# First stage of a two-layer kernel with its tiles started three ahead, small-tile mixing and logits, and GpSimd's bias after both sums of the tile before

## The reference

```
att   = softmax(mlp(cond))                 # 32 x 8, a small net on 128 values per batch
agg_w = sum_k att[b,k] * weight[k]         # a 64 x 64 mixing matrix for each batch
y     = agg_w @ x[b] + (att @ bias_k)      # mixes the 64 rows of a batch
g     = softmax(y @ gate_w.T)              # 8 routing weights for each row
u     = y * (g @ in_channel_scale)
x1    = x + u @ sign(weight).T * (g @ out_channel_scale) + bias
```

## Time and profile before

| | us |
|---|---|
| median of 3 runs | 580.35 (579.39 to 580.51) |
| the profiled execution | 579.01 |
| its span | 576.9 |

### The profile page before, as it was taken

The page is one execution under the profiler, slowest core; times in us unless marked ns, Lnnn a source line. Parts: engine busy times, 40 slices in busy tenths (PEclk is TensorE's granted clock), DMA queues, the critical chain, the costliest instruction groups (busy, mean ns, idle before and its releaser), DMA issues.

```text
span 576.9 us, 12309 instructions
## 1 busy us (share of the span) xinstructions
PE 562.8 (98%) x4917; PEld 491.0 (85%) x4917; DVE 253.1 (44%) x478; ACT 119.2 (21%) x271; POOL 148.3 (26%) x79
## 2 busy tenths in 40 slices
PE   4899999999999999999999999999999999999997
PEld 3778888888888889889889889899898898898896
DVE  4486567766676467242233222422422422323231
ACT  4723324323333233011010111111110110111100
POOL 0245555456453648011011011010110110110100
PEclk9999999999999999999999999999999999999999
DMA  8805333253333595223123043032131240330100
GB/s 333 324 36 164 111 119 118 86 178 92 112 118 111 158 192 151 78 39 110 45 77 113 32 83 105 9 114 82 32 114 52 61 114 36 77 111 9 68 36 36
DMA packets 36178, 58.22 MB, mean 101 GB/s; under 512 B 4096, under 2 KB 24384, under 8 KB 36160
## 3 DMA queue, kind: packets, MB, share of 16 engines
q1 hardware_dynamic: 36016, 57.70, 32.6%
q10 hardware_dynamic: 144, 0.26, 0.1%
HBM read 41.15 MB, written 16.79 MB: 100 GB/s over the span
## 4 chain that ended last, share of the span: by engine, by line
PE 93%; DVE 1%; ACT 0%; issue 0%
PE bank L503 50%; PE bank L430 20%; PE bank L482 8%; PE bank L383 4%; PE bank L392 4%; PE bank L538 4%; PE bank L406 1%; PE bank L398 0%; PE bank L531 0%; PE bank L412 0%; DVE weighted L738 0%; DVE agg L743 0%; DVE work L767 0%; DVE work L897 0%; ACT routing L617 0%; ACT gate L612 0%
## 5 line engine op out<-in xcount | busy, mean ns | idle before, releaser
L503 PE MATMUL bank<-early,parts 128*128 128x320 f32 (+1 forms) x1152 | 206.6, 337 | 0.0
L503 PEld LDWEIGHTS bank<-early,parts 128*128 128x128 f32 x1152 | 184.7, 188 | 16.6
L430 PE MATMUL bank<-late,parts 128*128 128x512 f32 x512 | 133.2, 407 | 1.8 <-ACT parts L628 1.5
L430 PEld LDWEIGHTS bank<-late,parts 128*128 128x128 f32 x512 | 92.6, 191 | 21.8 <-ACT parts L628 1.9
L954 POOL TENSOR_TENSOR work<-work,bias_bc 128x1024 f32<-128x1024 f32 x16 | 39.0, 2440 | 278.1 <-DMA work<-x_scratch 278.1
L503 PE MATMUL bank<-late,parts 128*128 128x512 f32 x384 | 94.3, 394 | 0.0
L503 PEld LDWEIGHTS bank<-late,parts 128*128 128x128 f32 x384 | 70.9, 188 | 16.1
L628 ACT ACTIVATE parts<-work 128x512 fp32r<-128x512 f32 x64 | 39.8, 632 | 102.3 <-DVE work L847 65.1
L922 POOL TENSOR_TENSOR work<-work 128x512 f32<-128x512 f32 x32 | 41.3, 1290 | 51.4 <-DVE work L803 51.4
L795 DVE TENSOR_TENSOR parts<-work,parts 128x512 fp32r<-128x512 f32 x64 | 46.6, 750 | 12.2 <-ACT parts L628 10.6
L914 POOL TENSOR_TENSOR work<-xs,bias_bc 128x1024 f32<-128x1024 f32 x16 | 38.8, 2428 | 47.4 <-ACT late L605 24.3
(11 more groups left out here) (89 smaller groups left out, 351.3 us busy)
## 6 DMA issues: line engine op xcount, KB each, us to landing
xs<-in_x SPq DMA_DIRECT2D x16, 512.0 KB, 3.8
x_scratch<-work SPq DMA_DIRECT2D x16, 512.0 KB, 3.0
raw<-x_scratch SPq DMA_DIRECT2D x128, 64.0 KB, 3.2
work<-x_scratch SPq DMA_DIRECT2D x16, 512.0 KB, 3.6
out_tokens<-work SPq DMA_DIRECT2D x15, 512.0 KB, 2.7
stage<-in_wearly SPq DMA_DIRECT2D x8, 576.0 KB, 3.8
row_bc<-token_rows_scratch SPq DMA_DIRECT2D x30, 64.0 KB, 3.6
work<-in_wsign SPq DMA_DIRECT2D x3, 512.0 KB, 10.9
```

The lines of the kernel that those rows point to most:

```text
L430: last = mm(bank[4 + h][:, :], parts[:, p, a, c, :], signs[:, c, h * HALF:(h + 1) * HALF], start=(k % 16 == 0), stop=(k % 16 == 15))
L503: return mm(dst, parts[:, p, a, c, :], w(b, c), start=(k == 0), stop=(close and k == 23))
```

## The change

- **Depth.** PE's period of tile t now does, in one block before step 18 (BLOCK_AT): logits of t+2, y of t+3, scales of t+1. The turn stands before step 7, the sum of the logits of t+2 before step 26. `y_t` has two buffers of its own. The first period is written out; DVE's and ACT's lists follow the new order, with mix_kernels four tiles ahead.
- **Small-tile mixing.** `agg` is 128 x 64: each batch's matrix on its 64 rows. product_y makes 32 matmuls of 64x64 with 64 columns (block c, batch b, column half g) in place of 8 of 128x128. Bank b now holds batch b, so the bias is added batch by batch. mix_kernels has one reduce.
- **Logits.** The gate, padded to 32 columns, is stationary; 128 columns of y_t move. Blocks c and c+4 go to the column tile c % 4, so bank 2 has four partial sums; ACT copies them (`logits_t`) and one matmul with the selection matrix C_SEL adds and turns them (`sum_logits`).
- **x again.** resid is loaded with x from DRAM (`load_again`) after x1 of two tiles before has been stored; add_bias0 works in place, and on POOL it stands after make_x1 of the tile before, both halves. make_x1 goes half by half.
- **Start.** The constants come in three transfers, one on ACT's queue; sign chunks, scales and x of tile 1 come in another order; SP's transfers around the first stage's end are put in another order (weight pieces, raw loads of the convolution, x1 of the last tiles).

The diff, cut to its core (of most parts only the new and the kept lines; what they replace stands in the functions above):

```diff
+TURN_AT, BLOCK_AT, SUM_AT, CONV0_AT = 7, 18, 26, 8
+SIGNS_FIRST = 4
...
+        agg = sb("agg", [P, 2, S])
...
+            load_consts(0, C_W0, C_W1)
             sp.dma_start(rws[:, :], rows).then_inc(rows_loaded, 16)
+            load_consts(2, C_GATE, C_END)
             load_x(0, 0)
+            for c in range(3):
+                load_sign(c)
             sp.dma_start(bias_bc[:, 0:HALF], scales).then_inc(scales_loaded, 16)
+            load_sign(3)
             load_x(0, 1)
+            for c in range(4, L8):
+                load_sign(c)
+            sp.wait_ge(tok_rows_ready, 2)
+            sp.dma_start(rows_dram.rearrange("a b s -> b a s"), tok_rows[:, :, :]).then_inc(rows_stored, 16)
+            def load_next(i, p, biased):
+                sp.wait_ge(y_biased, biased)
+                load_x(i, p)
+                load_row(aggb_row, i, p, aggb_loaded)
+            def load_again(i, p):
+                sp.dma_start(resid[:, p, :], tile_rows(x, 2 * i + p)).then_inc(x_again_loaded[p], 16)
+            sp.wait_ge(rows_stored, 16)
+            load_next(1, 0, 2)
+            for p in range(2):
+                sp.wait_ge(signs_ready, 7 + p)
+                load_again(0, p)
             sp.wait_ge(scale_ready, 1)
             sp.dma_start(bias_bc[:, :], bias0.broadcast_to([P, H])).then_inc(bias0_loaded, 16)
+            load_next(1, 1, 4)
...
+            def replace_x1(i, p):
+                store_x1(i, p)
+                sp.wait_ge(x1_stored[p], 16 * (i + 1))
+                load_again(i + 1, p)
+            def next_chunk(i):
                 sp.wait_ge(stage_hi[0], i + 1)
                 sp.wait_ge(stage_lo[0], i + 1)
                 load_stage(0, wearly[:, bass.ds(i + 1, 1), :].rearrange("p a n -> p (a n)"), NW)
+            with sp.Fori(0, PAIRS - 3) as i:
+                load_next(i + 2, 1, 4 * i + 8)
+                replace_x1(i, 0)
+                next_chunk(i)
+                load_next(i + 3, 0, 4 * i + 10)
+                replace_x1(i, 1)
+            late_i, last = PAIRS - 3, PAIRS - 1
+            load_next(last, 1, 4 * late_i + 8)
+            replace_x1(late_i, 0)
+            next_chunk(late_i)
+            replace_x1(late_i, 1)
...
+            replace_x1(last - 1, 0)
+            next_chunk(last - 1)
...
+            replace_x1(last - 1, 1)
             sp.wait_ge(xb_ready, 2 * TILES)
             sp.dma_start(bias_bc[:, :], bias1.broadcast_to([P, H])).then_inc(bias1_loaded, 16)
+            store_x1(last, 0)
+            store_x1(last, 1)
...
+            def inputs_of_y(i, p):
+                pe.wait_ge(x_loaded[p], 16 * (i + 1))
+                pe.wait_ge(agg_ready, 2 * i + p + 1)
             def product_y(i, p):
                 for c in range(L8):
+                    for b in range(2):
+                        for g in range(2):
+                            at = c * P + g * S
+                            rows = slice(b * S, (b + 1) * S)
+                            made = mm(bank[b][g * S:(g + 1) * S, c * S:(c + 1) * S], xs[rows, p, at:at + S],
+                                      agg[rows, p, :], start=True, stop=True)
+                        if c == L8 - 1:
+                            made.then_inc(y_done, 1)
+            def product_logits(i, p, first_tile=False):
+                pe.wait_ge(y_biased, 4 * i + 2 * p + 2)
+                if not first_tile:
+                    pe.wait_ge(gate_exp, 2 * i + p)
+                for c in range(L8):
+                    at = slice(EP * (c % 4), EP * (c % 4) + EP)
+                    made = mm(bank[2][at, 0:P], cst[:, C_GATE + c * EP:C_GATE + (c + 1) * EP], y_t[:, p, c, :],
+                              start=(c < 4), stop=(c >= 4))
+                made.then_inc(logits_made, 1)
+            def sum_logits(i, p, first_tile=False):
+                pe.wait_ge(logits_copied, 2 * i + p + 1)
+                if not first_tile:
+                    pe.wait_ge(u_ready, 4 * i + 2 * p - 1)
+                mm(bank[2][:, 0:E], logits_t[:, :], cst[:, C_SEL:C_SEL + E], start=True, stop=True).then_inc(logits_done, 1)
...
+            def period0(i, p, one, two=None, three=None):
                 for k in range(32):
                     if k == TURN_AT:
+                        turn_routing(*one)
+                    if k == BLOCK_AT:
+                        if three:
+                            inputs_of_y(*three)
+                        if two:
+                            product_logits(*two)
+                        if three:
+                            product_y(*three)
+                        product_scales(*one, copied=2 if two else 1)
+                    if k == SUM_AT and two:
+                        sum_logits(*two)
+                    ffn0_step(i, p, k)
+            for k in range(32):
+                if k == 6:
+                    pe.wait_ge(u_ready, 1)
+                    product_logits(0, 1)
+                if k == 10:
+                    inputs_of_y(1, 0)
+                    sum_logits(0, 1)
+                    product_y(1, 0)
+                if k == 16:
+                    turn_routing(0, 1)
+                if k == 22:
+                    inputs_of_y(1, 1)
+                    product_logits(1, 0)
+                    product_y(1, 1)
+                    product_scales(0, 1, copied=2)
+                if k == 28:
+                    sum_logits(1, 0)
+                ffn0_step(0, 0, k, True)
+            period0(0, 1, (1, 0), (1, 1), (2, 0))
+            with pe.Fori(1, PAIRS - 2) as i:
+                period0(i, 0, (i, 1), (i + 1, 0), (i + 1, 1))
+                period0(i, 1, (i + 1, 0), (i + 1, 1), (i + 2, 0))
             last_i = PAIRS - 1
+            period0(last_i - 1, 0, (last_i - 1, 1), (last_i, 0), (last_i, 1))
+            period0(last_i - 1, 1, (last_i, 0), (last_i, 1))
+            period0(last_i, 0, (last_i, 1))
...
+            def period0(i, p, one, two=None, chunk=None):
+                if one:
+                    round_routing(*one)
+                copy_out_scale(i, p, 1)
+                if chunk is not None:
+                    round_stage(0, NW, (chunk + 1) * 16, early[:, 0, bass.ds(chunk, 1), :].rearrange("p a n -> p (a n)"))
+                if two:
+                    copy_logits(*two)
+                if one:
+                    round_u(*one)
+                if two:
+                    gate_exps(*two)
+                    spread_routing(*two)
+                if one:
+                    copy_out_scale(*one, 0)
+            period0(0, 1, (1, 0), (1, 1), 0)
...
+                v.tensor_reduce(agg[:, p, :], weighted[:, :, :], AX.X, ALU.add).then_inc(agg_ready, 1)
...
+            add_mix_bias(0, 0, True)
+            dve.wait_ge(scale_hi, 1)
+            v.scalar_tensor_tensor(scale_w[:, :], bias_bc[:, 0:HALF], cst[:, C_SLO:C_SLO + 1], scale_w[:, :].bitcast(F32),
+                                   ALU.mult, ALU.add).then_inc(scale_ready, 1)
+            mix_kernels(0, 1)
+            route_max(0, 0)
+            route_sum(0, 0)
             split_routing(0, 0)
             scale_in(0, 0)
+            rest_of_u(0, 0, 0)
+            add_mix_bias(0, 1, True)
+            rest_of_u(0, 0, 1)
+            mix_kernels(1, 0)
+            route_max(0, 1)
+            route_sum(0, 1)
+            mix_kernels(1, 1)
+            add_mix_bias(1, 0)
+            split_routing(0, 1)
+            scale_out(0, 0, 0)
+            scale_in(0, 1)
+            rest_of_u(0, 1, 0)
+            route_max(1, 0)
+            rest_of_u(0, 1, 1)
+            route_sum(1, 0)
+            add_mix_bias(1, 1)
+            mix_kernels(2, 0)
+            def period0(i, p, before, one, two=None, three=None, four=None):
+                scale_out(*before, 1)
+                split_routing(*one)
+                if four:
+                    mix_kernels(*four)
+                scale_out(i, p, 0)
+                scale_in(*one)
+                rest_of_u(*one, 0)
+                if two:
+                    route_max(*two)
+                rest_of_u(*one, 1)
+                if two:
+                    route_sum(*two)
+                if three:
+                    add_mix_bias(*three)
+            period0(0, 1, (0, 0), (1, 0), (1, 1), (2, 0), (2, 1))
...
-            def add_bias0(i, p, first_tiles=False):
-                pool.wait_ge(x_loaded[p], 16 * (i + 1))
-                if not first_tiles:
-                    pool.wait_ge(x1_stored[p], 16 * i)
-                g.tensor_tensor(resid[:, p, :], xs[:, p, :], bias_bc[:, :], ALU.add).then_inc(xb_ready, 2)
-            def make_x1(i, p):
+            def add_bias0(i, p):
+                pool.wait_ge(x_again_loaded[p], 16 * (i + 1))
+                g.tensor_tensor(resid[:, p, :], resid[:, p, :], bias_bc[:, :], ALU.add).then_inc(xb_ready, 2)
...
+            def period0(before, now, chunk=None):
+                make_x1(*before, 1)
+                add_bias0(*now)
+                if chunk is not None:
```

(36 more changed lines are left out.)

293 lines of the change are left out of this document (112 added, 181 removed).

## The result

The changed kernel takes 559.3 us (median of 4 runs, 558.18 to 560.6) against 579.87 (4 runs): ratio 0.9667, 95% interval 0.9639 to 0.9694. Run again later on another chip beside the experiments it gave 0.9650 (0.9622 to 0.9678). I had predicted 556 and a range of 546 to 570. The profiled execution is 558.58, its span 556.5; before, 579.01 and 576.9: 20.4 less, where 24.2 were predicted.

What follows compares the result with a forecast made beforehand. PE, busy 98% of the span, bounds the kernel. First stage 52 + 11 x 10.04 + 8.9 + 8.05 + 10.2 + 2.0 = 191.6 us against 215.77, 24.2 less: 556 us, range 546 to 570.

Steps and rivals of the forecast that it cites:

- The block: PE's first-stage period with small-tile y and logits, sum, scales and gaps: 10.04 us against 11.84, 1.80 less; bounds 9.5 and 11.2.
- Why y is 1.0: Mixing product on PE: 16 instructions per quarter x (53 streaming + 9 leftover ns) = 1.0 us; bounds 0.85 and 1.42.
- Changes of shape: PE gaps between tile shapes: full to logits 0.30 us, logits to y 0.15, y to scales 0.12; bounds 0 and 0.3 each.
- The first feed-forward step: Start of the first stage: first feed-forward step at 26.7 us, against 26.31 before.
- Periods 0 and 1: First two tile periods: 13.6 and 11.3 us, together to 51.6, taken as 52; bounds 49 and 56.
- the wait of 1.2 for DVE: Period 0: PE waits 1.2 us for DVE's bias of tile 1 and mix of tile 2, on top of 12.35 of work.
- The steady tiles: Tiles 2 to 12 of the first stage: 11 periods of 10.04 us.
- Tile 13: First-stage tile without a y: 8.9 us.
- Tiles 14 and 15: Last first-stage tiles: 8.05 us for 14, which has no logits, and 10.2 for PE's 32 steps and convolution in 15.
- The end: Second stage waits 2.0 us (bounds 0 and 4): x comes late behind 16 raw loads, then bias and last chunk on POOL.
- That the others keep up: DVE's 7.4 us fits in 10.04; ACT slack 0.85 in chunk tiles, POOL at most 7.6 in a row, SP slack 2.6.
- slack 3.9: POOL's bias behind the predecessor's second sum: ACT's copy of the next out-scale to T+10.1, wanted by DVE at T+14.0; hidden.

Runs made afterwards that it cites:

- the other order: Changed kernel with the 32 small matmuls of y reordered, all 16 of one batch, then all of the other: ratio 0.9836 against the kernel before.
- the scales moved apart: Changed kernel with the scales at step 20, two feed-forward steps behind the block: 559.73 us, ratio 0.9679, against 557.95 of the change beside it.
- the move of x: Changed kernel with x1 of tile 13 stored and x of tile 15 loaded after the first eight raw loads, not all sixteen: 555.78 us, ratio 0.9596.
- the copy first: Changed kernel with ACT copying the logits before it rounds the weight chunk, in tiles that carry one: 563.45 us, ratio 0.9717.
- the bias first: Changed kernel with GpSimd's bias of a tile before the second sum of the tile before, not after both: 571.74 us, ratio 0.9862.

## Why the prediction was right, step by step

- *The block.* y 1.09 with its way to the scales (1.0 + 0.12 predicted), logits with the gap behind them 0.58 (0.46 + 0.15), gap ahead 0.32 (0.30), scales 0.59, sum 0.33 (0.24). Period 10.13 against 10.04, where the sum was mis-sized: the next step starts 0.33 after it, not 0.24. The whole gain per tile is 1.71 (11.84 to 10.13), where 1.80 was forecast. The runs that undid y and logits gave 0.88 and 1.00 per tile.
- *Why y is 1.0* was right in size only. I had 53 of streaming and 9 left over for each instruction of a quarter; the other order shows 55 in all with two quarters, so the 9 aren't a price per instruction but come with four at once. That the size was right is luck.
- *Changes of shape* cost what was said, and less when a short matmul has to end: shown by the scales moved apart.
- *The first feed-forward step*: 26.7 predicted, 26.83. *Periods 0 and 1*: 13.6 and 11.3 predicted, 15.6 and 11.6 measured (first step 26.83, tile 1 at 42.41, tile 2 at 54.05). Of the 4.0 us that the sum was off, 2.0 lie in these two. In period 0 the first six steps and the gap behind them take 2.86 us, where 1.63 is full speed, and logits, four steps and the sum up to 32.77 run slow too: 2.5 us in all, where I had added 0.4 for the low clock. In the trace of the change the granted clock reads 1.00 there. But in the run with the mixing product on the full array the same steps and logits take the same 2.86 and 1.01 us, after nearly the same idle time (1.63 and 1.66), and the record shows the low level, 0.50 (start and end us, length, busy us by engine, granted clock, DMA share, GB/s):

```profile
28.12:30.98 2.86, 2.86 (x7) 1.82 (x7) 2.86 (x5) 2.40 (x4) 0.00 (x0) 0.50 0.35 107
```

So it is the low level, 1.2 GHz, in both, and the step that was mis-sized is the 0.4. That no more than 2.0 are missing is in part luck: the wait of 1.2 for DVE that I had put into period 0 didn't come, and a gap of 0.55 that I hadn't put in did.
- *The steady tiles* 2 to 12: 111.55 against 110.4, 0.09 in each and 0.1 more at the turn in tile 2. *Tile 13* 9.56 against 8.9: without a y between them the scales wait for ACT's copy of the logits (the 0.68 in the row at 171.18), a wait that I hadn't seen. *Tiles 14 and 15* 8.16 and 10.23 against 8.05 and 10.2.
- *The end*: 2.0 predicted, 1.96 measured, and the move of x took it away. The transfers and GpSimd were as described; what ended last was DVE's rest of z, not GpSimd's rest of the chunk, 0.5 us later.
- *That the others keep up* was right in result, with less room than I wrote. I had taken DVE's and GpSimd's durations from the earlier trace rows as they stood, and both grew. GpSimd's order is no free choice, as I had costed it (slack 3.9): it closes a ring from the second sum over store and load to the next bias.

Sum: 54.05 + 111.55 + 9.56 + 8.16 + 10.23 + 2.04 = 195.6, against 191.6. Every part came out longer than forecast or equal, so the total owes nothing to errors that cancel between parts. The second stage is the same (360.9 from its first load to the end of the span, before 361.1).

## What to carry to other kernels

When PE is busy all the time, its time follows from the starts of its weight loads, and a change of tile shapes can be priced from any stage that has such tiles; add a gap for each change of shape (here 0.23 to 0.32 us behind 512 columns, 0.07 behind 64), and put small products together. On an engine that works in order, put the operation that waits for a far transfer behind those that release that transfer. Take slack on DVE and GpSimd from durations with both busy: here DVE's operations with two operands in SBUF grew from 0.69 to 1.05 us on the mean.

## What was not expected of the hardware

- Four 64x64 tiles in f32 come at 16 ns per instruction (64 in 1.02 us), two at 28 (64 in 1.77).
- DVE's 128x512 rest with two SBUF operands took up to 3.14 us beside GpSimd's operations, alone 0.68; those with a PSUM operand stayed between 0.67 and 0.69.
- In the straight-line code of period 0 PE stops in the middle of a y, between its 46th and 47th instruction (0.55 us, at 38.3), where no semaphore wait stands. In eight traces the 47th comes 11.8 to 12.0 us after the first feed-forward step, though that y begins 9.7 to 10.8 us after it, so the gap is 0.5 to 1.4 us: the earlier PE gets there, the longer it waits for something with a time of its own. What that is stays open. Where the gap was 1.39 (in the runs with the copy first and the bias first), the granted clock then fell to 0.50 for a time, and the stretch from 39.5 us to the next turn took 1.6 us longer.
- The record of the granted clock can miss the low level: 1.00 and 0.50 stand beside the same durations in two traces.
